# Output projection of two attentions in half precision: three passes over split parts in place of float32

## The reference

```python
attn = jax.nn.softmax(dots, axis=-1)
out = jnp.einsum('bhnm,bhmd->bhnd', attn, v)
out = out.transpose(0, 2, 1, 3).reshape(b, n, DIM)
return out @ wo.T + bo
```

## Time and profile before

| | us |
|---|---|
| median of 3 runs | 1390.16 |
| lowest and highest run | 1388.1, 1392.35 |
| profiled execution, time | 1392.13 |
| profiled execution, span | 1390.4 |
| busy: TensorE, VectorE, ScalarE, GpSimd | 1325.5, 1105.7, 693.2, 414.2 |

### The profile page before, as it was taken

The page is one execution under the profiler, slowest core; times in us unless marked ns, Lnnn a source line. Parts: engine busy times, 40 slices in busy tenths (PEclk is TensorE's granted clock), DMA queues, the critical chain, the costliest instruction groups (busy, mean ns, idle before and its releaser), DMA issues. The chain is left out here.

```text
span 1390.4 us, 37331 instructions
## 1 busy us (share of the span) xinstructions
PE 1325.5 (95%) x12290; PEld 1011.5 (73%) x12290; DVE 1105.7 (80%) x3711; ACT 693.2 (50%) x1639; POOL 414.2 (30%) x580
## 2 busy tenths in 40 slices
PE   6899999999999999999999999999999999998998
PEld 5677888755667777777655578878878888986666
DVE  7788778678889988888778877677664886678997
ACT  3566667544345555555434356676663233442331
POOL 2333336534443444447134432332330000000000
PEclk9999999999999999999999999999999999999999
DMA  5544445331333333334011243333346451660000
GB/s 168 156 121 125 123 140 173 86 118 47 84 104 100 89 90 91 86 92 124 28 57 47 72 115 99 97 92 90 103 137 171 162 174 43 162 144 15 16 15 23
DMA packets 134460, 138.16 MB, mean 99 GB/s; under 512 B 38985, under 2 KB 121676, under 8 KB 134220
## 3 DMA queue, kind: packets, MB, share of 16 engines
q1 hardware_dynamic: 134332, 136.51, 34.5%
HBM read 100.98 MB, written 35.48 MB: 98 GB/s over the span
## 5 line engine op out<-in xcount | busy, mean ns | idle before, releaser
L1155 DVE TENSOR_REDUCE negm<-ps 112x1 f32<-112x375 f32 x512 | 260.2, 542 | 106.2 <-PE ps L1279 104.2
L1279 PE MATMUL ps<-kst,qst 96*112 96x375 f16 x768 | 230.0, 332 | 10.1 <-DMA qst<-q_split 5.1
L865 ACT ACTIVATE p<-ps 125x448 f32<-125x448 f32 x336 | 177.1, 543 | 107.8 <-PE ps L1307 71.7
L834 POOL TENSOR_TENSOR qst<-m_row,diag 16x448 f16<-16x448 f16 x128 | 130.1, 1044 | 281.7 <-ACT m_row L944 276.7
L1294 PE MATMUL ps<-qst,kst 112*125 112x224 f16 (+1 forms) x1152 | 209.0, 263 | 3.9 <-ACT p L865 2.3
L1294 PEld LDWEIGHTS ps<-qst,kst 112*125 112x125 f16 (+1 forms) x1152 | 145.7, 137 | 37.6 <-issue 8.7
L1808 PE MATMUL ps<-fw,xs_e 128*128 128x512 f16 x672 | 158.9, 379 | 0.0
L1139 DVE TENSOR_SCALAR ps<-ps 125x448 f32<-125x448 f32 x192 | 120.1, 629 | 29.5 <-PE ps L1294 29.3
L1151 DVE CUSTOM_DVE_ANT_0 with_mask<-ps,mask_add 112x375 f16<-112x375 f32 x256 | 134.4, 545 | 9.3 <-issue 7.8
L1279 PEld LDWEIGHTS ps<-kst,qst 96*112 96x112 f16 x768 | 96.0, 129 | 36.9 <-DVE negm L1155 12.9
L1202 PE MATMUL ps<-wkv_split,ctxT 128*125 128x256 f16 x864 | 118.9, 274 | 0.2 <-DVE ks L1110 0.2
(11 more groups left out here) (264 smaller groups left out, 2608.9 us busy)
## 6 DMA issues: line engine op xcount, KB each, us to landing
k_split<-ks SPq DMA_DIRECT2D x48, 375.0 KB, 3.6
kst<-k_split SPq DMA_DIRECT2D x96, 187.5 KB, 2.9
fw<-in_w SPq DMA_DIRECT2D x16, 1024.0 KB, 7.3
qst<-q_split SPq DMA_DIRECT2D x96, 112.0 KB, 2.4
kst<-k_split SPq DMA_DIRECT2D x96, 93.8 KB, 2.7
stage<-in_ctxT SPq DMA_DIRECT2D x16, 375.0 KB, 4.0
rows<-x SPq DMA_DIRECT2D x48, 112.9 KB, 2.2
q_split<-qs SPq DMA_DIRECT2D x96, 56.0 KB, 2.6
```

What stands on the lines that cost most here:

```text
L834: pool.tensor_tensor(m_stack[q][m_rows, 4 * hg:4 * hg + 4, :], g.m_row[q][m_rows, :].rearrange("p (o s) -> p o s", o=1) .to_broadcast([n_m ...
L865: act.activation(p[p_of[hg]][kt], ps[0:KR, BK_ST + n % 2, 0:4 * S], ACT.Exp).then_inc(s_exp, 1)
L1155: dve.tensor_reduce(g.negm[1 - par][:, h:h + 1], scored, AX_X, ALU.max, negate=True).then_inc(s_max, 1)
L1279: mm = pe.matmul(ps[0:S, BK_S + h % 2, 0:SK], g.q_stack[q][0:96, h, :], g.k_stack[q][0:96, h // 2, :], start=True, stop=True)
```

## The change

In layers 0 and 2 the output projection becomes three half-precision passes. `oT` holds two half-precision parts, `[high, low]`, in the memory that was one float32 tile. ScalarE's copy in slot 14 writes the high part. A new step of VectorE, `output_low`, in slot 15 (between the maxima of heads 9 and 10) waits for that copy and writes `misc` less the high part as the low part. TensorE's `project_out`, still in slot 18, waits for this new step and not for ScalarE's copy, and runs six half-precision matmuls (three passes of two blocks) where two float32 ones stood. The weights get a split copy, `wo_split`: ScalarE writes the high part once at the end of pass 0, VectorE the low part in slot 0 of pass 1, after the maxima of heads 0 and 1. Layer 1 keeps its float32 matmuls; its ScalarE copy gets a wait on `s_wod`, the count of finished projections, that layers 0 and 2 get as well. Some semaphores are now made only in the stages that use them. The core of the diff:

```diff
@@ PLANS @@
-                v_out=[16, 20, 31], oT=14, m_out=26),
+                v_out=[16, 20, 31], oT=14, o_low=15, m_out=26),
@@ attention @@
+    WO_SPLIT = 3 if first else 1
+    oT = g.oT[:, :, :].rearrange("p c s -> p (c s)").bitcast(F16).rearrange("p (l c s) -> p l c s", l=2, c=KC)
+    wo_split = local.enter_context(nc.sbuf_tensor(f"wo_split{layer}", [128, 2, KC, D], F16))
@@ scalar @@
                     if on["o"] and s == plan.oT:
                         act.wait_ge(s_ob, i)
-                        act.activation(g.oT[:, :, :], misc[:, 0:KC * S].rearrange("p (c s) -> p c s", c=KC),
+                        at_least(act, s_wod, i - 1)
+                        act.activation(g.oT[:, :, :] if clipped else oT[:, 0, :, :], misc[:, 0:KC * S].rearrange("p (c s) -> p c s", c=KC),
                                        ACT.Copy).then_inc(s_oT, 1)
...
+                if not clipped and isinstance(i, int) and i == 0:
+                    act.wait_ge(s_w, 16 * (2 if first else n_w))
+                    step(act.activation(wo_split[:, 0, :, :], g.wo[:, :, :], ACT.Copy))
@@ vector @@
+            def output_low(i):
+
+                dve.wait_ge(s_oT, i)
+                at_least(dve, s_wod, i - 1)
+                dve.tensor_tensor(oT[:, 1, :, :], misc[:, 0:KC * S].rearrange("p (c s) -> p c s", c=KC),
+                                  oT[:, 0, :, :], ALU.subtract).then_inc(s_olow, 1)
...
+                    if not clipped and isinstance(i, int) and i == 1 and s == 0:
+                        dve.wait_ge(s_act, 3 if first else 1)
+                        dve.tensor_tensor(wo_split[:, 1, :, :], g.wo[:, :, :], wo_split[:, 0, :, :],
+                                          ALU.subtract).then_inc(s_wsplit, 1)
+                    if not clipped and on["o"] and s == plan.o_low:
+                        output_low(i)
@@ tensor @@
             def project_out(i):
-                pe.wait_ge(s_oT, i)
+                pe.wait_ge(s_oT if clipped else s_olow, i)
                 pe.wait_ge(s_bo_rows, 16 * 3)
-                if first and isinstance(i, int) and i == 1:
-                    pe.wait_ge(s_w, 16 * 2)
+                if not clipped and isinstance(i, int) and i == 1:
+                    pe.wait_ge(s_wsplit, WO_SPLIT)
                 pe.matmul(misc[0:S, 0:D], g.ones[:, :], g.bo_rows[:, :], start=True, stop=False)
-                for c in range(KC):
-                    mm = pe.matmul(misc[0:S, 0:D], g.oT[:, c, :], g.wo[:, c, :], start=False, stop=(c == KC - 1))
+                for l, r in ((0, 0),) if clipped else ((0, 0), (0, 1), (1, 0)):
+                    for c in range(KC):
+                        mm = pe.matmul(misc[0:S, 0:D], g.oT[:, c, :] if clipped else oT[:, l, c, :],
+                                       g.wo[:, c, :] if clipped else wo_split[:, r, c, :], start=False,
+                                       stop=(c == KC - 1 and (clipped or l == 1)))
                 mm.then_inc(s_wod, 1)
```

More of the change, by code:

```diff
@@ L463, in __init__ @@
     def __init__(self, turned, shift, scores, weigh, keys, low, rows, q, values, turn, divide, back, out, update, stats,
-                 maxima, pv, split, split_low, norm, xnT, q_out, k_out, v_out, oT, m_out):
+                 maxima, pv, split, split_low, norm, xnT, q_out, k_out, v_out, oT, o_low, m_out):
         at = lambda slots: {s: [n for n, x in enumerate(slots) if x == s] for s in sorted(set(slots))}
@@ L470, in __init__ @@
         self.update, self.maxima, self.pv, self.split, self.split_low = update, maxima, pv, split, split_low
-        self.norm, self.xnT, self.q_out, self.oT, self.m_out = norm, xnT, q_out, oT, m_out
+        self.norm, self.xnT, self.q_out, self.oT, self.o_low, self.m_out = norm, xnT, q_out, oT, o_low, m_out
         self.last_score = max(scores)
@@ L486 @@
                stats=[23, 26, 30], maxima=30, pv=0, split=30, split_low=16, norm=29, xnT=5, q_out=9, k_out=[1, 4],
-               v_out=[17, 20, 25], oT=16, m_out=31),
+               v_out=[17, 20, 25], oT=16, o_low=18, m_out=31),
 }
@@ L517, in attention @@
     s_wsplit = sem("w_split")
-    s_bvo = sem("bias_product")
-    s_bvo_sb = sem("bias_copied")
+    if biased:
+        s_bvo, s_bvo_sb = sem("bias_product"), sem("bias_copied")
     s_bo = sem("bias_parts")
@@ L523, in attention @@
         s_x_in = [sem(f"x_loaded{i}") for i in range(len(X_LOADS))]
+        s_ctx = [sem(f"ctx_loaded{i}") for i in range(2)]
+        s_ctx_hi, s_ctx_lo = sem("ctx_high"), sem("ctx_low")
         s_zero, s_zdram, s_ident, s_gates = (sem(n) for n in ("zeros", "zeros_in_dram", "ident", "gates_ready"))
@@ L526, in attention @@
     s_bo_rows = sem("bias_rows")
-    s_ctx = [sem(f"ctx_loaded{i}") for i in range(2)]
-    s_ctx_hi = sem("ctx_high")
-    s_ctx_lo = sem("ctx_low")
     s_xn = g.batch0.xn
@@ L562, in attention @@
     s_ob = sem("o_turned")
-    s_oT = sem("o_copied")
+    s_oT, s_olow = sem("o_copied"), sem("o_low")
     s_wod = sem("wo_done")
```

## The result

| | before | changed |
|---|---|---|
| median, us | 1390.63 (22 runs) | 1395.39 (22 runs) |
| profiled execution: time, span, us | 1392.13, 1390.4 | 1394.11, 1392.3 |
| ratio, with its interval | | 1.0031 [1.0022, 1.0041] |
| once more, on another chip: median, us | 1390.28 (17 runs) | 1396.35 (6 runs), 1.0051 [1.0031, 1.0071] |

The account below looks back on a forecast made before the run. TensorE was taken to set the pace of a pass, with VectorE having time to spare. Gains of 1.07 us in layer 0 and 1.93 in layer 2 took 1392.13 to 1389.1 us, 1387.2 on the median; range 1384 to 1393.5.

Parts of the forecast that it names:

- TensorE's saving: Projection in layers 0 and 2: six half-precision matmuls replace two float32 ones, saving 0.20 us per batch, at most 6.4 us.
- rival 2: Subtraction starts 0.25 us behind the copy, not 0.03: 1393; non-overlapping weight loads: 1390.7; chance 0.16 for both together.
- The subtraction: VectorE, before head 10: 0.39 us, starting 0.03 us behind the oT copy; bias rows' load 0.82 us behind copy's start.
- The steady passes: Gain per pass: 0.19 us in layer 0's loop (passes 5 to 10), 0.15 in layer 2 and layer 0's late passes.
- Head 10's late start: Layer 2: subtraction ends up to 0.05 us into head 10's slot; head 13 still gets 0.14 to 0.19 us earlier.
- Passes 2 and 4 of layer 0: Reciprocal-root pieces between the maxima push heads 10 and 11 back about 0.3 us: a loss of 0.1 us each.
- Pass 1: Layer 0: VectorE also makes the weights' low part, counted in full at 0.61 us, 0.1 gained later: -0.5 us.
- Pass 16: Last projection of layers 0 and 2 lies bare: 0.03 + 0.39 us added, 0.20 saved, -0.22 us each.
- Passes 11 to 15 stand like layer 2, 5 x 0.15 = 0.75: Late passes of layer 0: each gains 0.15 us as in layer 2, 0.75 us together.
- 15 x 0.15: Layer 2: fifteen passes gain 0.15 us each, 2.25 us together.
- Rival 3: VectorE isn't free when the copy lands, one more reduce precedes the subtraction: +0.3 us a batch, 1399; chance 0.12.
- The 0.12 for "slower": Chance of a measurement slower by more than about 0.3%, 4.2 us; it consisted of Rival 3 alone.

Follow-up runs that it names:

- e1: Changed kernel with float32 projections and no subtraction in passes 15 and 16 of layers 0 and 2; 1392.91 us against 1392.85 before, ratio 1.0009.
- e2: Changed kernel with float32 in pass 15 alone, pass 16 keeping the subtraction; 1392.48 us, ratio 0.9991.
- e7: Changed kernel with useless matmuls filling TensorE's wait in pass 15 (20 in layer 0, 4 in layer 2); 1393.42 us, ratio 1.0018.
- e8: Changed kernel with the reciprocal roots of pass 15 in slot 25 instead of 8, half precision in all passes; 1389.47 us, ratio 0.9992.
- e6: Kernel of e1, with the weights' low part made by GpSimd in pass 0, not VectorE in pass 1; 1388.73 us against 1390.47 before, ratio 0.9983.
- e10: The kernel of e6 run once more; 1388.93 us, ratio 0.9990 against before.
- e5: The kernel of e1 run again on another chip; 1388.51 us against 1390.47 before, ratio 0.9984.
- e4: Changed kernel with GpSimd making layer 1's mask diagonal in pass 11 of layer 0, not pass 15; 1395.64 us, ratio 1.0028 against before.

## Why the prediction was wrong, point by point

- **TensorE's saving: right.** Four records in 1.02 us became six in 0.82, the next scores are 0.22 and 0.21 us nearer. The loads, 132 ns each, hide under matmuls 109 ns apart: the half of rival 2 that was about loads falls. The fast weight load, which by the Trainium skill (TensorE: Matmul & The Clock Gate, Weight-path perf modes) these loads lack, isn't needed at this spacing: L1252 and the value projections of the earlier trace rows take the same 0.82 us for six.
- **The subtraction: right.** Forecast 0.39 us and 0.03 us behind the copy; measured 0.388 us over 32, and 0.03 us in pass 16 and in layer 2. In layer 0's loop it starts 0.12 us behind the copy's end. The load came at 0.92 and 0.83 us behind the copy's start (forecast 0.82), and none of it cost anything. Rival 2 falls. (Its chain adds up to 1.04 us, not the 1.02 written there; nothing hangs on it.)
- **The steady passes: mechanism right, size too small.** I took 0.19 us a pass in the loop and 0.15 in layer 2 and the late passes of layer 0; measured 0.18 to 0.20 as a mean over the loop, 0.18 over passes 11 to 14 and 0.18 over passes 2 to 14 of layer 2 (single passes there 0.12 to 0.27 in the first two profiles). Head 10's late start was not waited for. Passes 2 and 4 of layer 0, for which I had a loss of 0.1 us each, gain 0.20 each (15.05 to 14.85). Pass 1 lost 0.53 us (forecast 0.5), with the weights' low part at 0.79 us and not 0.61.
- **Pass 16: right.** Forecast -0.22 us a layer; e1 against e2: 0.22 and 0.21 to 0.23.
- **"Passes 11 to 15 stand like layer 2, 5 x 0.15 = 0.75", and "15 x 0.15" in layer 2: the step that failed.** Pass 15 is none of them. I had read where `in_between` puts its steps in passes 1 to 4, and not that it also has a block for the last pass, in slot 8, ahead of the new slot 15. The change adds a wait, and I named what is queued behind the waiting instruction; what is queued ahead of it I read in steady passes and in passes 1 to 4 alone. Forecast 0.15 us gained in each; measured, beside pass 16's 0.2, 6.7 us lost in layer 0 and 1.0 in layer 2.
- **Rival 3 had the mechanism and the wrong place.** "VectorE isn't free when the copy lands" was priced as 0.3 us in each of 32 passes and argued away by the steady passes. It happened in two of them, with 5.09 and 1.16 us of wait where 0.45 and 0.54 were priced. The 0.12 for "slower" stood on 32 small waits, so it doesn't count as having seen this. The row that would have shown it was in the trace of before: the root step at 271.22 us with 1.65 us and VectorE busy 4.83 us of the 5 from 270 on, while TensorE was busy 4.69 of them.
- **The clock was in no term.** The wait of 1.16 us cost 1.0 us; the one of 5.09 us was followed by a granted clock of 0.62 and 0.69 and cost 2.0 to 2.7 us more (e7).
- **The ways back.** Undoing pass 15 alone (e2), moving the roots (e8) or both last passes (e1) takes the loss away. The best version, e6 and e10, is faster than the changed kernel by 7 us and than before by 0.1 to 0.2% at most: 0.9983 [0.9972, 0.9993] and 0.9990 [0.9979, 1.0001]. The first interval shows a gain on before, the second just misses one.

## What to carry to other kernels

A new wait on an engine's queue is to be checked in every pass that differs from the steady one, the first and the last above all: list what stands ahead of the new instruction in each. Here, work for the next stage had been put into the last pass because nobody waited for it there; the first instruction that somebody does wait for inherits all of it. A second point is about measuring: a gain of 0.3% read off the stretches of one execution is not yet a gain of the kernel (e1, e5, e6, e10). And where a change gains some 4 us in steady passes, a single wait of 5 us with the clock falling behind it is more than the gain.

## What the hardware showed

- **Small VectorE steps beside GpSimd.** Steps on 128x10 take 0.17 us alone (e4, e8) and 1.08, 1.65 and 1.75 us beside GpSimd: they end at 266.44, 268.40 and 270.39, each 0.03 us after the end of GpSimd's memset or select (266.41, 268.37, 270.36). In the trace of before the step of 1.65 us ends at 272.87 and GpSimd's select at 272.84. Not slowed down, then, but held until the other ends. The Trainium skill (SBUF — State Buffer, Who interferes with whom) states it so: the pair of ports that the two share is an exclusive lock, and the later one blocks fully. The rows agree. It holds, the page says, for VectorE's two-port modes, or for two SBUF inputs against a GpSimd instruction that reads SBUF. The step at 265.36 has one input and is held by a memset, so it would have to be in a two-port mode, which no row shows.
- **The clock.** TensorE, working at 2.4 GHz until 268.1 us and then without a matmul for 4.87 us, was granted 1.2 GHz (0.50) for the matmuls behind, 272.9 to 278 us (256 columns: 1.49 us for six instead of 0.82). The waits of 1.16 us in layer 2 and 1.12 us in e4 left the clock at 1.00, those of 1.59 us in e6 and 2.99 us in e4 were followed by 0.53 (227.5 to 231 us) and 0.73 (240 to 245). The length of the last wait alone doesn't decide: at the end of the program the same wait of 0.96 us was followed by 0.62 in some kernels and 1.00 in others.
- **A stage can change its length without being changed.** The expert stages, whose code is the same, took up to 2 us more, in a pattern that came back from run to run of one kernel (112.2 and 112.5 us for e6 and e10, 110.1 to 110.7 for before). In e1 and e5 they are 1.8 us longer than before, of the 4.3 us that the steady passes gained. The cause isn't shown.
